# Second layer: width neighbours from shifted copies in place of a matrix product

## The reference, cut to what matters

```
yp_x = pad(y, width, 1, mode='reflect')
lap_x = yp_x[:, :, :-2] - 2.0 * y + yp_x[:, :, 2:]
lap_y = the same along the other axis
du_dt = zX * lap_x + zY * lap_y + zR * y * (1.0 - y)
```

## Time and profile before

| what | us |
|---|---|
| median of 3 runs (2438.74 to 2442.45) | 2442.35 |
| profiled execution, whole | 2440.37 |
| its span, first to last instruction | 2438.6 |
| TensorE matmul busy in the span | 2262.9 (93%) |
| VectorE busy | 1840.2 (75%) |
| ScalarE busy | 1291.7 (53%) |
| GpSimd busy | 1005.2 (41%) |

### The profile page before, as it was taken

One profiled execution on the slowest core, in us unless ns is written; L12 is line 12 of the kernel. 1 busy time (PEld: TensorE's weight loads), 2 busy tenths in 40 slices (PEclk: granted clock), 3 DMA queues, 4 the chain that ended last, 5 costly groups with the idle time before them and its releaser, 6 DMA issues.

```text
span 2438.6 us, 53844 instructions
## 1 busy us (share of the span) xinstructions
PE 2262.9 (93%) x18368; PEld 2057.9 (84%) x18368; DVE 1840.2 (75%) x5132; ACT 1291.7 (53%) x3839; POOL 1005.2 (41%) x1063
## 2 busy tenths in 40 slices
PE   4788989999887799999999999899999999999999
PEld 3677878778776688888888887799999999999999
DVE  5778787777878666666666665588868888888876
ACT  1666666666663455555555555434325555555522
POOL 5435445354444455555555554133322222222073
PEclk8999999999998899999999999899999999999999
DMA  4523323233240312212212113131226767777443
GB/s 138 177 87 102 107 88 109 86 99 107 82 129 3 82 38 56 51 44 56 50 45 57 47 47 85 28 79 36 45 73 226 233 229 234 237 230 236 146 121 124
DMA packets 196341, 259.23 MB, mean 106 GB/s; under 512 B 58646, under 2 KB 168486, under 8 KB 185318
## 3 DMA queue, kind: packets, MB, share of 16 engines
q1 hardware_dynamic: 187206, 237.13, 32.0%
q0 software_dynamic: 8864, 18.66, 3.0%
HBM read 176.10 MB, written 43.94 MB: 90 GB/s over the span
## 4 chain that ended last, share of the span: by engine, by line
PE 61%; DVE 15%; ACT 8%; POOL 7%; issue 6%; DMA 1%; POOLq 0%; SPq 0%; DVEq 0%; ACTq 0%
PE bank L55 51%; PE bank L136 6%; ACT Ph L654 2%; POOL P L1786 2%; ACT Ph L656 2%; PE bank L1296 1%; DVE Ph L815 1%; ACT PTh L666 1%; PE bank L1336 1%; DVE xe L921 1%; DVE sgs L945 1%; PE bank L399 1%; POOL Qn L1811 1%; POOL Qn L1809 1%; DVE hb L955 1%
## 5 line engine op out<-in xcount | busy, mean ns | idle before, releaser
L1490 ACT ACTIVATE P<-P,mx 128x144 f32<-128x144 f32 x512 | 206.2, 405 | 263.8 <-DVE mx L1611 262.9
L55 PE MATMUL bank<-xD_hi,w1e_lo 128*128 128x256 f32 x880 | 251.1, 285 | 0.0
L2623 POOL DMA_INDIRECT xE<-d_y,ixs x78 | 111.2, 1426 | 336.3 <-PE bank L136 300.8
L55 PE MATMUL bank<-w2e_hi,hrD_hi 128*128 128x256 f32 x880 | 249.0, 283 | 0.0
L55 PE MATMUL bank<-w2e_lo,hrD_hi 128*128 128x256 f32 x880 | 248.9, 283 | 0.0
L55 PE MATMUL bank<-w2e_hi,hrD_lo 128*128 128x256 f32 x880 | 248.9, 283 | 0.0
L1786 POOL TENSOR_TENSOR P<-P,rs 128x512 f32<-128x512 f32 x128 | 133.1, 1040 | 273.9 <-DVE rs L1620 270.4
L55 PE MATMUL bank<-xD_lo,w1e_hi 128*128 128x256 f32 x880 | 245.9, 279 | 0.0
L55 PE MATMUL bank<-xD_hi,w1e_hi 128*128 128x256 f32 x880 | 245.6, 279 | 0.0
L2232 ACT ACTIVATE hD<-bank,b1E 128x256 f32<-128x256 f32 x312 | 127.0, 473 | 197.2 <-PE bank L55 188.1
L1120 POOL TENSOR_TENSOR xe<-xe 128x704 f32<-128x704 f32 (+3 forms) x64 | 88.2, 1378 | 340.5 <-DVE xe L926 340.3
(11 more groups left out here) (324 smaller groups left out, 7922.3 us busy)
## 6 DMA issues: line engine op xcount, KB each, us to landing
w1raw<-in_ew SPq DMA_DIRECT2D x39, 1024.0 KB, 6.0
w2raw<-in_ew SPq DMA_DIRECT2D x39, 1024.0 KB, 4.9
stack<-d_rot SPq DMA_DIRECT2D x256, 96.0 KB, 2.7
K<-Kn SPq DMA_DIRECT2D x256, 72.0 KB, 2.1
d_rot<-QKh SPq DMA_DIRECT2D x64, 256.0 KB, 3.1
Q<-Qn SPq DMA_DIRECT2D x256, 64.0 KB, 2.0
d_ys<-oE SPq DMA_DIRECT2D x39, 256.0 KB, 2.6
d_rot<-QKl SPq DMA_DIRECT2D x32, 256.0 KB, 2.9
```

What stands on the lines that cost most here:

```text
L55: inst = e.matmul(out, l, r, start=k == 0, stop=k == len(pairs) - 1)
L1490: inst = e.activation(P1[t % 2][:, n, :], P1[t % 2][:, n, :], ACT.Exp, bias=mx1[t % 2][:, 2 * g + sg:2 * g + sg + 1], scale=-1.0, accum_ou ...
L2623: e.indirect_dma_start(out=xE[q % 2][c], out_offset=None, in_=d_y, in_offset=bass.IndirectOffsetOnAxis(ap=ixs[r % 4][:, c:c + 1].bitcast(U ...
```

## The change

The width neighbours come by DMA. sync_c gets neighbours(b): eight copies within the on-chip memory. Four write y moved down by one partition into `near` (the tile that held the matrix), four write y moved up by one into `fu`; the single-partition copies carry the chunk boundary and the reflected edge. GpSimd adds them (near = near + fu) behind the division of slot 7; for batch 0 VectorE does. The term -2y of both axes goes into the constant: zs[2] becomes zR - 2 zX - 2 zY, by two instructions on 16 columns once, so L1672 goes. L1683 reads near in place of the bank. laplace, its matrix, its load and its semaphore go. In slot 7 VectorE waits for g_near before it overwrites fu. project(b+1, 3) waits only for an old rotation, and category of the last two batches for an older product (v_mul).

```diff
+            def neighbours(b):
+                if not 0 <= b < B:
+                    return
+                y = X[:, b]
+                e.wait_ge(v_xf, b + 1)
+                if b:
+                    e.wait_ge(v_t7, b)
+                    e.wait_ge(v_rn, 2 * b)
+                for dst, src in ((near[1:113], y[0:112]), (near[113:128], y[112:127]),
+                                 (near[0:1, 1, :], y[127:128, 0, :]), (near[0:1, 0, :], y[1:2, 0, :]),
+                                 (fu[0:112], y[1:113]), (fu[112:127], y[113:128]),
+                                 (fu[127:128, 0, :], y[0:1, 1, :]), (fu[127:128, 1, :], y[126:127, 1, :])):
+                    e.dma_start(dst, src).then_inc(l_near, 16)
...
+            neighbours(0)
...
+            neighbours(1)
...
                     stack(b, half)
+                    if half == 0:
+                        neighbours(b + 2)
...
                 elif n == 3:
-                    if b + 1 < B:
-                        e.wait_ge(v_t7, b + 2)
-                    else:
-                        e.wait_ge(v_x1r, 8 * b + 1)
+                    e.wait_ge(v_x1r, 8 * b + 1)
...
-                    if s == 1:
-                        laplace(entering(b))
...
                 e.tensor_scalar(fa, y, zN, zR, ALU.mult, ALU.add).then_inc(*vs.up())
+                e.wait_ge(g_near, b + 1)
                 e.tensor_tensor(fu[:, :, 1:255], y[:, :, 0:254], y[:, :, 2:256], ALU.add)
...
                 e.tensor_tensor(fa, fa, y, ALU.mult).then_inc(*vs.up())
-                e.scalar_tensor_tensor(out=fu, in0=y, scalar=-2.0, in1=fu, op0=ALU.mult, op1=ALU.add).then_inc(*vs.up())
...
-                e.wait_ge(p_lap, b + 1)
-                e.scalar_tensor_tensor(out=fa, in0=lap_bank(b), scalar=zX, in1=fa, op0=ALU.mult, op1=ALU.add
+                e.scalar_tensor_tensor(out=fa, in0=near, scalar=zX, in1=fa, op0=ALU.mult, op1=ALU.add
                                        ).then_inc(v_t7, 1)
...
+            def add_neighbours(b):
+                if not 0 < b < B:
+                    return
+                e.wait_ge(l_near, LNEAR + 128 * (b + 1))
+                e.tensor_tensor(near, near, fu, ALU.add).then_inc(g_near, 1)
+                e.wait_ge(g_near, b + 1)
...
                     normal(t)
+                    if s == 7:
+                        add_neighbours(entering(b + 1))
```

More of the change, by code:

```diff
@@ L505, in category @@
                 else:
-                    e.wait_ge(v_t7, 1)
+                    e.wait_ge(v_mul, 4 * b - 1)
                 for st in range(2):
@@ L1186, in program @@
         tile("space0", 32)
-        lap, rot1 = tile("lap", 2, 256), tile("rot1", 3, 256)
+        near, rot1 = tile("near", 2, 256), tile("rot1", 3, 256)
         fa, fu, rn1 = tile("fa", 2, 256), tile("fu", 2, 256), tile("rn1", 256)
@@ L1213, in program @@
         l_st, LST = [[l_x[0], l_x[1]], [l_x[2], l_wa]], [[16, 16], [16, 128]]
-        p_S1, p_T1, p_PV1, p_qk1, p_V1, p_lap, p_one, p_back = (sem(f"p_{n}") for n in (
-            "S1", "T1", "PV1", "qk1", "V1", "lap", "one", "back"))
+        p_S1, p_T1, p_PV1, p_qk1, p_V1, p_one, p_back = (sem(f"p_{n}") for n in (
+            "S1", "T1", "PV1", "qk1", "V1", "one", "back"))
+        g_near = sem("g_near")
+        l_near, LNEAR = l_rw, 96 * B
         v_mx1, v_ri1, v_PT1, v_O1, v_t7, v_rn, v_xn, v_x1r, v_back, v_w1 = (sem(f"v_{n}") for n in (
@@ L1230, in entering @@
             return b + 2 if b >= -1 else B
-        def lap_bank(b):
-            return halves(0 if b else 5)
         def sums_bank(b):
@@ L1239, in sync_c @@
         def sync_c(e):
+            def neighbours(b):
[11 more added lines that the diff above has]
+                    e.dma_start(dst, src).then_inc(l_near, 16)
             e.wait_ge(p_v, B)
             e.wait_ge(g_rot, 2 * B)
-            for dst, src in ((lap, "lap"), (gn, "gn"), (rot1, "rot1k")):
+            for dst, src in ((gn, "gn"), (rot1, "rot1k")):
                 e.dma_start(dst, a[src]).then_inc(l_c, 16)
@@ L1409, in back @@
                     for f in range(8)]).then_inc(p_back, 1)
[L1411 to L1423, removed]
             def squares(b):
@@ L1441, in pe_c @@
                         project(b + 1, 0)
-                    if b == -3 and s == 0:
-                        laplace(0)
                     if b == -3 and s == 4:
                         squares(0)
-                    if s == 1:
-                        laplace(entering(b))
                     if s == 2:
@@ L1659, in differences @@
                 else:
-                    e.wait_ge(s_v, vs.n)
+                    e.wait_ge(l_near, LNEAR + 128)
+                    e.tensor_tensor(near, near, fu, ALU.add).then_inc(g_near, 1)
+                e.wait_ge(s_v, vs.n)
                 e.tensor_scalar(fa, y, zN, zR, ALU.mult, ALU.add).then_inc(*vs.up())
+                e.wait_ge(g_near, b + 1)
                 e.tensor_tensor(fu[:, :, 1:255], y[:, :, 0:254], y[:, :, 2:256], ALU.add)
@@ L1722, in split_back @@
                                 wo1[0][:, f:f + 2, :].bitcast(F32), ALU.subtract).then_inc(v_w1, 1)
-            e.wait_ge(l_c, 96)
+            e.wait_ge(l_c, 80)
             e.tensor_scalar(zs[:, 3, :], zs[:, 2, :], -1.0, None, ALU.mult).then_inc(*vs.up())
+            for i in range(2):
+                e.wait_ge(s_v, vs.n)
+                e.scalar_tensor_tensor(out=zs[:, 2, :], in0=zs[:, i, :], scalar=-2.0, in1=zs[:, 2, :], op0=ALU.mult,
+                                       op1=ALU.add).then_inc(*vs.up())
             for b in range(-3, B + 1):
@@ L1911, in program @@
         WE = WD + 3
-        LD, LW, LP, LO = 96, 32, 32, 16
+        LD, LW, LP, LO = 80, 32, 32, 16
         ZEROED, READY = 3, 4
@@ L2733 @@
     A["w_gate"], A["w_up"], A["w_down"] = g["L0_ffn_w_gate"], g["L0_ffn_w_up"], g["L0_ffn_w_down"]
-    lap = np.zeros((256, 256), np.float32)
-    for w in range(256):
-        lap[w, w] -= 2.0
-        lap[w, 1 if w == 0 else w - 1] += 1.0
-        lap[w, 254 if w == 255 else w + 1] += 1.0
-    A["lap"] = T2(np.ascontiguousarray(lap.T))
     A["gn"] = g["L1_attn_g_norm"].reshape(2, 128).T
```

## The result

The changed kernel takes 2443.88 us (median of 12 runs, 2442.58 to 2447.83), the kernel before 2440.72 in the runs beside them (2436.42 to 2445.69): a ratio of 1.0021, 95% interval 1.0013 to 1.0029. Forecast was 2431.0. The profiled execution took 2444.61, its span 2442.5. Eleven microseconds of gain were forecast, three of loss came.

A forecast was written before the change was run, and what follows sets the result against it. GpSimd and VectorE, not TensorE's busy time, were taken to bound slots 1 and 2. Steady batches 14 x 0.68 = 9.5 us plus overlap 1.6 gave 11.1 off, forecast 2431; own range 2425 to 2436, 8 in 10 for 2424 to 2440.

The forecast's parts named there:

- the steady batch: Slots 1 and 2 of batches 2 to 15: each batch 0.68 us shorter, bounds 0.3 to 1.03, 9.5 us in all.
- The rule of the Trainium skill: Slot 1: GpSimd operations and VectorE ones with two on-chip inputs exclude each other throughout; 0.68 stands, nearer 0.85 if bandwidth is shared.
- the overlap: Stretch where the two layers overlap: 1.3 - 1.6 + 1.9 = 1.6 us gained, between 5 gained and 4 lost.
- the copies and the addition in slot 7: SP's copies between the stacks and GpSimd's addition behind slot 7's division: cost nothing, copies with about 8 us of cover.
- The rival's mechanism: Slower: copies landing after 1146.66 hold GpSimd's addition, then VectorE's shifted sum and maxima; 18 us lost, 2460; chance 0.08.
- Batch 0: In the overlap: L1672's 2.15 us goes, which VectorE's maxima waited behind; gain 1.3, bounds 2.1 and -1.
- Batch 1: In the overlap: shifted sum L1662 waits for GpSimd's addition behind L1135; a loss of 1.6 us, bound 0.
- The end: End of the overlap: project(0, 3) moves into TensorE's idle time, the turning gains up to 2.3 us, 1.9 taken.
- VectorE has its rotations to finish: End of the overlap: the reason given for taking 1.9 us of gain in place of up to 2.3.
- No change: Rival: steady batches gain 0.3 us or less as L1671 or another late instruction holds, overlap gives nothing; 2438 to 2444; chance 0.17.

The follow-up runs named there:

- e12: e11 with combine(b+1, 0) moved behind slot 1's division in the loop proper only; 16.7 us faster than the kernel before, 5.8 faster than e11.
- e6: Kernel before, product kept, with the eight copies of batches 2 to 15 added, half as wide or less, into an unread tile; 2457.58 us, ratio 0.9993.
- e8: e2 with six copies a batch in place of eight, those of 112 and 15 rows joined into 127; 2567.05 us, ratio 1.0440.
- e3: Changed kernel with eight unread products on TensorE where the products of batches 0 and 1 stood; 2442.57 us, ratio 1.0013.
- e15: e13 with eight unread products at the places of batches 0 and 1, no padding there; 4.8 us faster than e13.
- e16: e14 and e15 together; 7.6 us faster than e13.
- e4: Changed kernel with batch 1's addition of the shifted copies on VectorE in place of GpSimd; 2441.42 us, ratio 1.0008.
- e14: e13 with batch 1's addition of the shifted copies on VectorE, not GpSimd; 2.7 us faster than e13.
- e1: Changed kernel run once more, unaltered; 2443.84 us, ratio 1.0015 to the kernel before.
- e13: Changed kernel with 16 satisfied waits on TensorE at each of the 16 places of the product; if anything slower than e1, no time given.
- e2: Changed kernel with the old product for batches 0 and 1 and the copies for batches 2 to 15; 2433.51 us, ratio 0.9979.
- e7: e2 with combine(b+1, 0) moved behind slot 1's division on GpSimd's queue; 2440.64 us on a slower chip, ratio 0.9925.
- e10: e2 run again, unaltered, on one chip with e11; ratio 0.9983.
- e17: Kernel before with 260 satisfied waits (130 instructions) on TensorE ahead of its first product; ratio 1.0009.
- e5: e2 with 16 satisfied waits on TensorE where the product of batches 2 to 15 stood; 2439.92 us on a slower chip, ratio 0.9916.
- e11: e5 run again, unaltered, on one chip with e10; 6.5 us faster than e10.
- e18: e2 with 252 satisfied waits (126 instructions) on TensorE ahead of its first product; ratio 0.9913.

## Why the prediction was wrong, point by point

**Right: the steady batch.** 0.68 was forecast, 8.7 us over the 13 batches from 853 to 1450 is 0.67. Each instant stands where it was put: the division binds slot 1, the idle time is 1.33, L1671 is held, no wait ahead of project(b+1, 3). The rule of the Trainium skill that was weighed there ("SBUF — State Buffer", section "SBUF: two separate sides") fits only roughly: shut out until GpSimd's end, L1671 would end its full 0.68 behind it, and it ended 0.54 behind here and 0.56 in the overlap. e12 shows the limit more clearly: from 1100.34 to 1103.43 VectorE did work that takes 2.18 us alone and GpSimd, inside it, work of 1.46, which together is more than the 3.09 that passed. There the two engines shared; they didn't exclude each other for whole instructions.

**Right: the copies and the addition in slot 7.** e6's offset grows by 0.1 us over the whole steady part. In the changed kernel SP issues them from 1132.31 to 1137.7, and GpSimd's addition comes at 1147.41. The rival's mechanism was real, as e8 shows; its condition wasn't met with copies of 112 and 15 rows.

**Wrong: the overlap, "1.6 gained, between 5 gained and 4 lost"; measured 5.7 and 5.4 lost.** With the last part (below) this is nearly all of the difference: 7.3 us here and 7.9 there, of the 15 between forecast and trace. By its terms:
- Batch 0, "gain 1.3, bounds 2.1 and -1": 2.0 and 1.7 lost. VectorE's queue did get free earlier, but the step left out what the product did for TensorE besides computing: without it the granted clock of 700 to 735 is 0.80 and not 0.95. e3 and e15 put 3.1 and 3.3 us on that, e16 only 1.0.
- Batch 1, "a loss of 1.6": 3.5, from 760 to 790 in the table. Right in kind, and half of what came: L1662 ended 3.8 late, 2.3 of which it had brought along, so 1.5 as forecast; the rest was lost in what stands behind it. Moving the addition to VectorE, where it still takes 1.77, gives back 2.3 to 2.6 (e4, e14, e16).
- The end, "I take 1.9": 0 from 790 to 853. The turning did gain 2.3 (5.0 late at 787, 2.7 at 804), but it was given back within 6 us. TensorE's next products wait 1.55 for VectorE's rotation and run at half clock:

```profile
803.33 1.12 PE L55 MATMUL bank<-fu,ones 128*128 128x256 f32 x4 [0.19 <-DVE tb L1649]
```

```profile
807.47 2.04 PE L55 MATMUL bank<-fu,ones 128*128 128x256 f32 x4 [1.55 <-DVE tb L1646]
```

(before above, after below). The clause "VectorE has its rotations to finish" was there, and priced at 0.4.

**Missing: the last part.** The sum had no term for code that the change doesn't touch, and 7 to 8 us were lost there. Its cause isn't settled. Shown is: it's in every trace of a changed kernel that has copies for batches 0 and 1, padded or not (changed, e1, e3, e4, e13 to e16), in e2, e7, e8 and e10, and, on chips where before takes 2459 or more, also in before with copies or with 130 instructions added (e6, e17); it's absent or 2.7 us in all four with the old product for two batches and 112 or 126 instructions added on TensorE (e5, e11, e12, e18), on three chips. So instructions added on TensorE can remove it. Neither their number nor TensorE's place in a loaded piece decides: e11 and e12 have as many rows of TensorE as e15 and e16, which have the stretch, and e2 stands nearly at before's place and has it. e11 and e13 differ in VectorE's, GpSimd's and SP's programs too. Whether the engines lack instructions there, and what would hold these up, was not shown; no recorded load was in flight in the changed kernel's gap. Had the last part stayed as it was, the overlap's loss would have left the changed kernel 3.8 to 5 us faster than before (the offsets at 1600), about 2436 to 2437: inside "2424 to 2440", at or just above the end of "2425 to 2436".

**The rival that gave the number.** The measured time lies in the range of "No change", 2438 to 2444, but not by its mechanism: it had the steady batch shrink by 0.3 or less and the overlap give nothing. The batch gave its 0.67, and it was taken back by two losses that had no term (the clock's in batch 0 and the last part's) and by one that was too small (batch 1).

## What to carry to other kernels

TensorE's work in a stretch where it is often idle isn't free to remove: look at the granted clock of that stretch, and price the products behind it at both levels. In steady batches, price a removed product by the engine that releases the next one, not by its own length, then look what that engine does first (here one combine, worth another 0.5 us a batch). And a change in the number of instructions can move time in code that it doesn't touch: compare the two traces by offset to the end before explaining a median, and try the same change with some instructions added that do nothing. Count them in the trace: 16 waits were 8 rows, and the padding here put back less than half of what the product had. It removed the stretch in one version (e10 to e11) and not in another (e13).

## What the runs showed of the hardware that was not expected

- A DMA of 127 partitions of 2 KB moved at 25 to 29 GB/s, with about one of the 16 DMA engines busy (share 0.07), and one of 112 landed in 2.6 us; two such copies in place of four cost 7.9 us a batch (e8 against e2).
- Eight rows of products whose result is not read, at 704 us, made later products faster: the clock of 711 to 719 stayed at 1.00, and 3.1 and 3.3 us were won (e3, e15). In e16 that clock was 0.79, and 1.0 us was won.
- All engines but GpSimd stopped together for 4.2 us without a wait between them (changed kernel; 0.5 to 2.7 at a time in other traces); 112 added instructions of TensorE removed the stretch in one version (e10, e11: 6.5 us), 128 didn't in another (e13).
- The same kernel takes 2438.5 us on one chip and 2462.5 on another; e6's trace on one of the slower loses 8.2 of its 17 us in that stretch, and 9.4 more between 2300 and 2430. All six traces of the two slower chips lose between 2300 and 2430 (5.5 to 11.8 us: e5 to e8, e17, e18), none of the others does. Why is not known.
